# An embedding-mean projection on one core: from the fourth tile's join on, products leave PSUM by VectorE alone

## The chip, the cores and the metric

One core of a Trainium2 chip. The metric is the device time of one execution in microseconds (us); shorter is better. The same core runs everything, so there is no talk between cores.

## The reference

1024 users have 200 item ids each. An id below 12500 is valid; the embedding rows (512 floats) of the valid ids are summed, divided by their number, and the mean goes through a projection with a bias.

```python
valid = sequence_ids < emb_table.shape[0]              # (1024, 200), table (12500, 512)
seq_emb = emb_table[where(valid, sequence_ids, 0)] * valid[..., None]
user_repr = seq_emb.sum(axis=1) / maximum(valid.sum(axis=1, keepdims=True), 1.0)
logits = user_repr @ proj_w + proj_b                   # proj_w (512, 12500), out (1024, 12500)
```

## The kernel before, in words

**Tiles, blocks, units.** The users are 8 tiles of 128; the weights are 25 blocks of 500 columns. A tile times a block is one product, here a unit; there are 200, numbered 0 to 199 in the order in which every engine walks through them (list `units`). The tiles join one after another: tile 0 starts alone at unit 0, and the others join at units 11, 24, 38, 55, 70, 87 and 104 (`joined`, from the argument `JOIN`). A tile that joins begins with the last five blocks that are still there, since five blocks are held at a time (`SPLIT`).

**One unit on TensorE** (lines 839 to 860). Twelve matmuls of 128x128 by 128x500 into one of six PSUM banks (`acc`, unit r uses bank r modulo 6): high halves of mean and weight, then low weight with high mean, then high weight with low mean (`part` 0 to 2, four matmuls each). The first unit of a tile waits for `s_mean_hi` at its start and for `s_mean_lo` ahead of part 2 (lines 844 to 848). A unit first waits until the bank of unit r - 6 is free (`wait_moved`, line 842).

**How a product leaves.** The list `by_act` says for each unit which engine carries it from PSUM to the staging area (`stage`, eleven slots). The two ways differ:

```python
by_act = [r < joined[ACT_TILES] or r < joined[BOTH_TILES] and r % 2 == 0 for r in range(UNITS)]
```

- `by_act[r]` true: TensorE runs a thirteenth, short matmul (line 858) that adds the bias from its three bf16 parts, and ScalarE copies the bank (`move_out`, line 421).
- false: no thirteenth matmul; VectorE adds the bias from `bias_sb` while it copies (`move_out`, line 648). `bias_sb` holds five blocks' biases, each loaded by its own DMA (`load_bias`, line 303) after the last move on VectorE that used its slot (`late_last`).

With `ACT_TILES` 1 and `BOTH_TILES` 5, ScalarE carries units 0 to 10 and then the even ones up to 68: 40 in all.

**VectorE's order is written out by hand** (the loop over `r` in the vector block). For each r: the move of unit r if it is VectorE's; after a join the rest list of the next tile (`fill_slots`); the low halves of a weight block (`w_low`, line 633, two instructions); then the columns of the next tile that are due at r. A tile has 26 columns: gathered embedding rows that are added into `sums` (`add_column`, lines 566 and 569), numbered 0 to 25 here. `column_due` spreads them from joined[t-1] - 2 to joined[t] - t - 3. Between columns stand the sorting rounds of the tile after it (after columns 1, 5, 9, 13 and 17), the rare further sums with their branch after column 20 (`sum_further`), and `choose` after column 19. At joined[t] - 3 comes `mean_of(t)` (line 615), at joined[t] - 2 `mean_low(t)` (line 620). Because the first three columns of the tile after it are due at joined[t] - 2, they and a sorting round stand ahead of `mean_low(t)`.

**TensorE's other steps.** `sum_rest(t)` at joined[t] - 3 (line 794), `turn(t)`, the transposition of the mean (line 774), at joined[t] - 1, after `mean_of(t)`; `list_rest` after the join (lines 786 to 788).

**ScalarE** also rounds the weights to their high halves (`w_high`, line 430), the means (`mean_high`, 446), and scales the rests (`rest_share`, 457).

**GpSimd** gathers the rows by indirect DMA (line 361) into twelve slots. Each pair of gathers waits until the columns that used their slots are added, and, from tile 2 on, for the move of a unit:

```python
if t > 1 and column_due(c) > GATHER_LEAD:
    wait_moved(pool, column_due(c) - GATHER_LEAD - 1)
```

So the first pair of tile 5 waits for the move of unit 47, the first pair of tile 6 for the move of unit 62. `wait_moved` counts the moves of the engine that carries the unit, so it waits for that engine's earlier moves too.

**SyncE** issues the stores (one per unit, line 309), the weight loads (line 297) and the bias loads, in the order of r; each waits on that one queue. From block 16 on there are two slots for raw weights: the load of block 20 follows `w_low(18)`.

Of the kernel before, what the change touches and what calls it, by code (L numbers as in the profile page):

```python
# [5 lines left out]
def mean_embedding_projection(nc, ids, table, proj, bias, out, FAST=26,  # L6
# [24 lines left out]
    RAW_MORE, MORE_LOADS = 2, 16  # L31
    OTHERS_FIRST = 7
    FURTHER_BEHIND, LIST_FIRST_AT, BIAS_DUE = 20, 21, 3
    ACT_TILES, BOTH_TILES = 1, 5
    PART_AT = (0, 32, 64)
    BIAS_ROWS = PART_AT[-1] + NB
    COLS = FAST * TILES
# [845 lines left out]
```

## Time and profile before

| | us |
|---|---|
| median of 3 runs | 633.22 (633.05 to 634.0) |
| the profiled execution | 632.95 |
| its span, first to last instruction | 631.1 |
| TensorE busy (matmuls) | 607.6 (96%) |
| VectorE busy | 407.2 (65%) |
| ScalarE busy | 146.2 (23%) |
| GpSimd busy | 232.2 (37%) |

The profiled execution's own time is its span and some 1.9 us around it. Busy matmul time counts overlapping instructions; the granted clock was 1.00 of full speed, which is the 2.4 GHz level, in all but the start of the span (mean 0.997). Instructions on one engine can overlap by a tenth of a microsecond, so what one costs its engine is best read from start to start. "Idle before" is what the engine waited ahead of an instruction, and for whom.

### The profile page before, as it was taken

Reading aid. Unit: us, or ns where it says so; the run is one execution under the profiler, and the core shown is the slowest. Engines: PE = TensorE matmul, PEld = TensorE weight load, DVE = VectorE, ACT = ScalarE, POOL = GpSimd, SP = SyncE. Lnnn points to the kernel's source line nnn. Section 1 sums busy time; section 2 is a strip of 40 time slices with the busy share of each in tenths; the row PEclk is TensorE's granted clock in tenths of the full one; section 3 lists DMA queues with packets and bytes.
Section 4 is the critical chain, followed back from the end, with each engine's and each line's share of the span. In section 5 each row is a group of like instructions: output and inputs, shape, how many; then the busy total and the mean of one; then the engine's idle time right before and its main releaser. Section 6 shows DMA issues by size and latency. Waiting matters only on the chain.

```text
span 631.1 us, 7599 instructions
## 1 busy us (share of the span) xinstructions
PE 607.6 (96%) x2604; PEld 477.1 (76%) x2604; DVE 407.2 (65%) x721; ACT 146.2 (23%) x163; POOL 232.2 (37%) x227
## 2 busy tenths in 40 slices
PE   1989999999999999999999999999999999999997
PEld 0337657778788777788888888888888888888886
DVE  7988978889896699598698455433333333343442
ACT  8917425132132131120020023111000112111210
POOL 5777877777574377664475000000000000000000
PEclk9989999999999999999999999999999999999999
DMA  9979999999899589888688349935455555566632
GB/s 307 386 259 341 385 393 399 375 320 292 291 319 327 193 279 321 266 251 284 210 285 316 139 133 309 311 120 176 157 179 180 179 169 173 188 186 212 212 112 98
DMA packets 77703, 158.31 MB, mean 251 GB/s; under 512 B 9287, under 2 KB 65042, under 8 KB 77658
## 3 DMA queue, kind: packets, MB, share of 16 engines
q1 hardware_dynamic: 60378, 110.30, 51.0%
q0 software_dynamic: 17280, 47.47, 22.5%
q8 instruction: 21, 0.34, 0.2%
q14 instruction: 24, 0.20, 0.1%
HBM read 115.70 MB, written 51.20 MB: 264 GB/s over the span
## 4 chain that ended last, share of the span: by engine, by line
PE 89%; DVE 5%; DMA 3%; issue 1%; ACT 0%; POOL 0%; POOLq 0%; DVEq 0%
PE acc L853 82%; PE turned L802 4%; DMA rows<-in_L_rec_emb_table_dram,index 3%; DVE sums L569 1%; PE acc L858 1%; DVE w_lo L633 1%; PE turned L794 1%; PE turned L774 0%; DVE top L522 0%; DVE key L526 0%; DMA ids_sb<-in_r_sequence_ids_dram 0%; DVE count L660 0%; ACT w_hi L430 0%; PE turned L788 0%; POOL rows L361 0%
## 5 line engine op out<-in xcount | busy, mean ns | idle before, releaser
L361 POOL DMA_INDIRECT rows<-in_L_rec_emb_table_dram,index x208 | 222.4, 1069 | 101.9 <-issue 60.8
L853 PE MATMUL acc<-w_hi,mean_hi 128*128 128x500 f32 x800 | 224.1, 402 | 0.8 <-ACT mean_hi L446 0.8
L648 DVE TENSOR_TENSOR stage<-acc,bias_sb 128x500 f32<-128x500 f32 x160 | 107.3, 676 | 173.8 <-PE acc L853 173.2
L853 PE MATMUL acc<-w_hi,mean_lo 128*128 128x500 f32 x800 | 213.6, 388 | 0.7 <-DVE mean_lo L620 0.7
L853 PE MATMUL acc<-w_lo,mean_hi 128*128 128x500 f32 x800 | 214.1, 389 | 0.0
L853 PEld LDWEIGHTS acc<-w_hi,mean_lo 128*128 128x128 f32 x800 | 150.3, 188 | 32.1 <-DVE mean_lo L620 1.2
L853 PEld LDWEIGHTS acc<-w_hi,mean_hi 128*128 128x128 f32 x800 | 150.2, 189 | 32.0 <-issue 4.3
L853 PEld LDWEIGHTS acc<-w_lo,mean_hi 128*128 128x128 f32 x800 | 150.3, 188 | 31.5
L569 DVE SCALAR_TENSOR_TENSOR sums<-rows,mask,sums 128x512 f32<-128x512 f32 x165 | 124.2, 753 | 19.5 <-issue 7.3
L430 ACT ACTIVATE w_hi<-w_raw 128x2000 fp32r<-128x2000 f32 x39 | 72.9, 1876 | 220.1 <-PE acc L853 197.7
L633 DVE TENSOR_TENSOR w_lo<-w_raw,w_hi 128x1000 fp32r<-128x1000 f32 x74 | 85.3, 1195 | 13.1 <-ACT w_hi L430 13.1
L421 ACT ACTIVATE stage<-acc 128x500 f32<-128x500 f32 x40 | 23.2, 586 | 93.6 <-PE acc L858 93.6
L457 ACT ACTIVATE mean<-turned,inv_count 128x512 f32<-128x512 f32 x7 | 4.8, 689 | 73.8 <-PE turned L794 65.5
L802 PE MATMUL turned<-rows,diags_at_hi 128*128 128x512 f32 x30 | 15.7, 679 | 1.6 <-DMA rows<-in_L_rec_emb_table_dram,index 1.6
L858 PE MATMUL acc<-bias_parts,pick 89*128 89x500 bf16 x40 | 15.4, 386 | 0.0
L522 DVE MAX8 top<-key 128x8 f32<-128x200 f32 x40 | 14.7, 367 | 0.8
L526 DVE MATCH_REPLACE8 key<-top,key 128x200 f32<-128x200 f32 x40 | 14.3, 358 | 0.0
L802 PEld LDWEIGHTS turned<-rows,diags_at_hi 128*128 128x128 f32 x30 | 6.3, 219 | 10.3 <-issue 6.6
L808 PE MATMUL acc<-many,ones_b 128*128 128x16 bf16 x1 | 0.2, 193 | 12.4 <-DVE stage L667 12.4
L802 PE MATMUL turned<-rows,diags_at_lo 128*128 128x512 f32 x22 | 11.8, 685 | 0.1
L802 PE MATMUL turned<-rows,diag 128*128 128x512 f32 x20 | 9.9, 620 | 1.8 <-DMA rows<-in_L_rec_emb_table_dram,index 1.0
L858 PEld LDWEIGHTS acc<-bias_parts,pick 89*128 89x128 bf16 x40 | 4.1, 102 | 10.0 <-issue 10.0
(106 smaller groups left out, 187.9 us busy)
## 6 DMA issues: line engine op xcount, KB each, us to landing
out_dram<-stage SPq DMA_DIRECT2D x200, 250.0 KB, 3.8
w_raw<-in_L_rec_proj_w_dram SPq DMA_DIRECT2D x39, 1000.0 KB, 7.5
bias_sb<-in_L_rec_proj_b_dram SPq DMA_DIRECT2D x39, 250.0 KB, 5.8
raw_at_hi<-in_L_rec_proj_w_dram SPq DMA_DIRECT2D x4, 1000.0 KB, 14.1
rows<-in_L_rec_emb_table_dram,index POOLq DMA_INDIRECT x208, 6.2
raw_at_lo<-in_L_rec_proj_w_dram SPq DMA_DIRECT2D x3, 1000.0 KB, 16.5
stage<-in_L_rec_proj_w_dram SPq DMA_DIRECT2D x1, 1000.0 KB, 26.1
ids_sb<-in_r_sequence_ids_dram SPq DMA_DIRECT2D x1, 700.0 KB, 4.4
```

Of the source, the lines that this page charges most:

```text
L361: return pool.indirect_dma_start(out=dst, out_offset=None, in_=table, in_offset=bass.IndirectOffsetOnAxis(ap=column, axis=0), bounds_check ...
L421: nc.scalar.activation(stage[:, g % STAGE, r - stores[g][0]], acc[:, r % BANKS, 0:BW], ACT.Copy).then_inc(s_moved_by_act, 1)
L430: nc.scalar.activation(w_hi[:, q % SPLIT], raw(q), ACT.Copy).then_inc(s_w_hi, 1)
L522: dve.max(eight, key[:]).then_inc(s_sort, 1)
L526: dve.match_replace(key[:], eight, key[:], -1.0).then_inc(s_sort, 1)
L569: dve.scalar_tensor_tensor(sums[:], rows[:, c % ROWS], mask[:, t, j:j + 1], sums[:], ALU.mult, ALU.add).then_inc(s_summed, 1)
L633: low = dve.tensor_tensor(w_lo[:, q % SPLIT, at:at + half], raw(q)[:, at:at + half], high, ALU.subtract)
L648: dve.tensor_tensor(stage[:, g % STAGE, r - stores[g][0]], acc[:, r % BANKS, 0:BW], bias_sb[:, i % BIAS], ALU.add).then_inc(s_moved_by_dve, 1)
L794: nc.tensor.matmul(turned[:], placed[:, t % PLACED], rest_rows[:], start=t > 0, stop=t >= len(ON_PE)).then_inc(s_rest, 1)
L802: nc.tensor.matmul(turned[:], diagonal_of(c), rows[:, c % ROWS], start=j == 0, stop=j == FAST - 1).then_inc(s_added, 1)
L853: last = nc.tensor.matmul(bank, first, second, start=part + k == 0, stop=part == 2 and k == K - 1 and not by_act[r])
L858: last = nc.tensor.matmul(bank, pick[:, q % NB:q % NB + 1].to_broadcast([BIAS_ROWS, P]), bias_parts[:], start=False, stop=True)
```

## The change

`BOTH_TILES` goes from 5 to 3. The list `by_act` is now false from joined[3] = 38 on instead of from joined[5] = 70 on. The sixteen even units 38, 40, ... 68 lose their thirteenth matmul (line 858) and are carried by VectorE (line 648) instead of ScalarE (line 421). All waits on their moves go to VectorE's counter, those of TensorE, GpSimd and SyncE alike. Three entries of `late_last` change too, and with each the unit at which a bias load is issued: the bias of block 18 goes from unit 27 to 38, of block 20 from 31 to 40, of block 22 from 37 to 56. The number of bias loads stays 39.

```diff
-    ACT_TILES, BOTH_TILES = 1, 5
+    ACT_TILES, BOTH_TILES = 1, 3
```

## Rows read from the trace of the kernel before

**Rows 1.** The page: the chain that ended last by line; the bias matmul's group.
```profile
PE acc L853 82%; PE turned L802 4%; DMA rows<-in_L_rec_emb_table_dram,index 3%; DVE sums L569 1%; PE acc L858 1%; DVE w_lo L633 1%; PE turned L794 1%; PE turned L774 0%; DVE top L522 0%; DVE key L526 0%; DMA ids_sb<-in_r_sequence_ids_dram 0%; DVE count L660 0%; ACT w_hi L430 0%; PE turned L788 0%; POOL rows L361 0%
...
L858 PE MATMUL acc<-bias_parts,pick 89*128 89x500 bf16 x40 | 15.4, 386 | 0.0
```

**Rows 2.** The chain in order of time: start, length, what (us).
```profile
75.99 1.00 POOL rows L361
...
77.30 6.83 DMA rows<-in_L_rec_emb_table_dram,index
...
183.36 0.23 PE acc L858
...
363.49 264.27 PE acc L853 x1164
```

**Rows 3.** VectorE's timeline up to tile 4's join: start, length, what [idle before].
```profile
177.72 0.22 DVE L584 TENSOR_SCALAR rank<-turned,own_slot 128x1 f32<-128x1 f32 x1 [0.19 <-PE turned L788]
...
195.18 2.31 DVE L633 TENSOR_TENSOR w_lo<-w_raw,w_hi 128x1000 fp32r<-128x1000 f32 x2 [4.92 <-ACT w_hi L430]
...
211.30 0.67 DVE L648 TENSOR_TENSOR stage<-acc,bias_sb 128x500 f32<-128x500 f32 x1
211.89 2.46 DVE L569 SCALAR_TENSOR_TENSOR sums<-rows,mask,sums 128x512 f32<-128x512 f32 x3
214.26 1.26 DVE L648 TENSOR_TENSOR stage<-acc,bias_sb 128x500 f32<-128x500 f32 x2
216.38 0.75 DVE L615 SCALAR_TENSOR_TENSOR mean<-sums,inv_count,mean 128x512 f32<-128x512 f32 x1 [0.86 <-ACT mean L457]
221.29 0.68 DVE L648 TENSOR_TENSOR stage<-acc,bias_sb 128x500 f32<-128x500 f32 x1 [4.16 <-PE acc L853]
221.89 0.75 DVE L566 TENSOR_SCALAR sums<-rows,mask 128x512 f32<-128x512 f32 x1
222.74 0.76 DVE L569 SCALAR_TENSOR_TENSOR sums<-rows,mask,sums 128x512 f32<-128x512 f32 x1
...
226.40 0.68 DVE L620 TENSOR_TENSOR mean_lo<-turned,mean_hi 128x512 fp32r<-128x512 f32 x1
```

**Rows 4.** The same view up to tile 5's join.
```profile
254.75 0.67 DVE L648 TENSOR_TENSOR stage<-acc,bias_sb 128x500 f32<-128x500 f32 x1
...
257.71 1.26 DVE L648 TENSOR_TENSOR stage<-acc,bias_sb 128x500 f32<-128x500 f32 x2
263.86 0.68 DVE L648 TENSOR_TENSOR stage<-acc,bias_sb 128x500 f32<-128x500 f32 x1 [4.89 <-PE acc L853]
...
269.80 0.68 DVE L620 TENSOR_TENSOR mean_lo<-turned,mean_hi 128x512 fp32r<-128x512 f32 x1
```

**Rows 5.** TensorE's timeline, the two joins.
```profile
221.03 0.60 PE L774 MATMUL turned<-ident,mean 128*128 128x128 f32 x4
...
227.13 1.19 PE L853 MATMUL acc<-w_hi,mean_lo 128*128 128x500 f32 x4 [0.74 <-DVE mean_lo L620]
...
266.31 0.39 PE L858 MATMUL acc<-bias_parts,pick 89*128 89x500 bf16 x1
...
271.53 1.08 PE L853 MATMUL acc<-w_hi,mean_lo 128*128 128x500 f32 x4
```

**Rows 6.** GpSimd's timeline: first gathers of tile 5 and of tile 6.
```profile
212.95 1.00 POOL L361 DMA_INDIRECT rows<-in_L_rec_emb_table_dram,index  x1 [8.99 <-DVE sums L569]
...
251.50 1.00 POOL L361 DMA_INDIRECT rows<-in_L_rec_emb_table_dram,index  x1 [0.30 <-issue]
```

**Rows 7.** Landing of single gathers: those begun at 212.95, 214.26, 215.56, and 307.83.
```profile
DMA to landing us min/median/max: 3.5/3.5/3.5
...
DMA to landing us min/median/max: 4.4/4.4/4.4
...
DMA to landing us min/median/max: 5.4/5.4/5.4
...
DMA to landing us min/median/max: 5.5/5.5/5.5
```

**Rows 8.** A stretch with its busy times; last columns: granted clock, DMA share, GB/s.
```profile
183.00:195.00 12.00, 12.00 (x54) 9.46 (x53) 7.08 (x12) 2.32 (x2) 8.37 (x8) 1.00 0.98 351
```

## The prediction, made blind

> **What bounds the kernel now.** I read the chain that ended last first [rows 1]: 82% of it is TensorE's product matmuls. The reader should see there that TensorE is the bound, and that the bias matmul has its own 1%, so it is on the path and not under something. The chain in order of time [rows 2] gives its price: 0.23 us each, 0.227 from start to start (183.36 to 183.59). The 386 ns mean in its group is a pipelined length, not a cost. From 363.49 on the chain is one piece of product matmuls, so what is gained or lost before that reaches the end unchanged, unless a later join adds a wait. Then I read the engine that receives the work, VectorE [rows 3, 4]. It is 65% busy over the span, but what counts is what it does just before tiles 4 and 5 join. TensorE's timeline [rows 5] shows that at tile 4's join it already waits 0.74 us for the low mean, and at tile 5's it does not. Last I read the gathers [rows 6, 7], because their pacing hangs on the moves that change engine.
>
> **The credit.** Sixteen bias matmuls go: 16 x 0.227 = 3.63 us. Nine of them (units 38 to 54) lie before tile 4's join, 2.04 us, seven (56 to 68) between it and tile 5's, 1.59 us. ScalarE loses sixteen copies; it mostly waited for TensorE there, so I cost that at nothing. Should a weight rounding have waited behind a copy, it comes earlier.
>
> **The debit on VectorE.** A move costs it 0.59 us, start to start (211.30 to 211.89 [rows 3]). A column sum directly after another starts 0.85 later, anything else 0.66 later, so a move put between two sums costs only 0.39. Sixteen moves are about 9 us of VectorE, 2.5 times the credit. Whether they matter depends on where VectorE waited.
>
> *Up to tile 4's join.* Moves 38 and 40 fall ahead of the 4.92 us wait at 195.18 [rows 3], which absorbs their own time. But that wait ends with the load of block 20, which is issued after the low halves of block 18, and these now stand behind move 38. The rest list waited 0.19 for TensorE and an instruction may overlap a sum's end by 0.10, so 0.59 - 0.29 = 0.30 us is passed on. Bound below: 0, if the load does not mind. Bound above: the DMA share is 0.98 there at 351 GB/s [rows 8], and two bias loads of 250 KB move towards this stretch while one leaves it: 0.7 us for one, 1.0 in all. I take 0.30, as the first comes 5 us ahead of the load of block 20 and the second behind it.
>
> From there moves 42, 44 (each between two sums) and 46 come ahead of move 47: 0.39 + 0.39 + 0.59 = 1.37. Move 47 goes from 211.30 to 212.97. Then 48 (0.39), 50 and 52 (0.59 each): the mean of tile 4, which could have started at 215.44 and waited until 216.38, starts at 215.44 + 0.30 + 1.37 + 0.39 + 1.18 = 218.68 and ends at 219.43. TensorE finishes unit 53 eight bias matmuls early, at 221.03 - 1.82 = 219.21 [rows 5], so the transposition waits 0.2 us. This alone would be cheap: the 4.16 us that VectorE waited before move 53 are used up, no more.
>
> *The gathers.* The first gather of tile 5 started 0.98 after the end of move 47 (211.97 to 212.95 [rows 6]), so now at 214.62; the next ones follow every 1.30. A row can be used 1.30 after its gather's start (1.00 on GpSimd, then the transfer [rows 2]) plus the landing time. With the landings of these very gathers, 3.5 and 4.4 us [rows 7], the rows are there at 219.42 and 221.62. VectorE reaches column 0 at about 219.9 (move 53, then 0.59) and column 1 at 220.8, where it waits until 221.62. From column 1 to the low mean it needs 226.40 - 222.74 = 3.66 us for sort and sum, so the low mean starts at 225.28. The third row (5.4 us) is there in time. TensorE resumes 0.73 after its start (226.40 to 227.13): 226.01 instead of 227.13. **1.12 us are saved of 2.04 at tile 4's join.** With landings of 5.4 throughout it would be 0.1; with 3.5 throughout 1.96.
>
> *Up to tile 5's join.* VectorE starts 1.12 early. Moves 54, 56, 58 and 60 put move 61 at 254.75 - 1.12 + 2.36 = 255.99 [rows 4]. **Here the pacing changes.** The first gather of tile 6 waits for the move of unit 62, which ScalarE made before; the gather ran at 251.50 [rows 6], without being held up. Now the move stands in VectorE's order, after move 61 and two sums: 255.99 + 0.59 + 0.85 + 0.66 = 258.09, its end 258.76, the gather 259.74. That is 8.2 us later, so tile 6's rows arrive just when VectorE wants them. VectorE itself: after moves 62 to 66 it reaches move 67 at 258.89 - 1.12 + 2.36 + 0.39 + 1.18 = 261.70, where it had waited 4.89; then mean, then move 68 when unit 68 ends, 266.31 - 1.12 - 1.36 = 263.83, plus the 0.27 that such a start lags: 264.10. Column 0 could start at 264.69, column 1 at 265.54. With 4.4 us for the second gather, the row is there at 259.74 + 2.60 + 4.4 = 266.74. The gather at 307.83 is the nearer case, since it too follows a long pause and a run of moves whose stores go out together; it took 5.5 [rows 7], which gives 267.84. The low mean starts 3.66 later, 271.50, and TensorE resumes part 2 at 272.23 instead of 271.53 [rows 5]: **0.70 us later than before**, against 0.40 earlier with 4.4. I take 0.6. Later joins had their order on VectorE before, so nothing is added there, and the end moves with this.
>
> The sum against the profiled execution: 632.95 + 0.6 = 633.55. The median of the runs shown is 0.27 above the profiled one, so the forecast is 633.8. What can be told from no change is about 0.2% (1.3 us), so this is "same", leaning slower.
>
> **A rule of the skill at this point.** The row says 3.5 to 5.5 us landing for a gather of 256 KB. The Trainium skill, "DMA: Bandwidth & Descriptors", section "Anatomy of one DMA — SWDGE (gpsimd) path", fits such a transfer as 2.0 us plus its bytes over 436 GB/s; an estimate from that page is 2.6 us, and by it no row would be late. The trace does not agree: its shortest quoted landing is 0.9 above that.
>
> **Rivals.**
>
> *The rows come in time.* All landings 3.5 us. Tile 4's join saves 1.96; the gather of tile 6 then starts at 258.90, its second row is there at 265.00, hardly after VectorE, which makes unit 68's move at 263.26 and could reach column 1 at 264.70; the low mean follows at 268.66 and TensorE at 269.39: 2.1 us faster, 631.1. For it: the first gather after a pause did take 3.5. Against: the second and third took 4.4 and 5.4. The page's fit would give the same outcome as this rival. The full 3.63 (629.6) would need VectorE to be ahead as well; its order excludes it at tile 5, as the low mean stands behind move 68. Chance 0.17.
>
> *Slower: rows and load late.* The load of block 20 lands 0.7 later still, and the second gathers take 5.4. Tile 5's gather starts at 215.32, its second row is there at 223.32, TensorE resumes at 227.71 (0.58 later); tile 6's gather then starts at 261.44, its second row is there at 269.44, TensorE resumes at 273.83: 2.3 us slower, 635.5. It decides once landings pass 5 us at both joins. For it: the stores of the moves that come in a run now leave together, beside the gathers. The Trainium skill, same page, section "SWDGE vs HWDGE vs iDMA", says that each DMA engine goes round-robin between the two kinds of queue; no row here shows the turns themselves. Against: the DMA queues are nearly empty before tile 5's first gather. Landings near 7 us, as in the start-up [rows 2], would make it about 5 us. Chance 0.30.
>
> *The work was hidden anyway*, so nothing moves and there are no new waits. Against it speaks the bias matmul's own share of the chain. Chance 0.03; the time would be 633.2.
>
> **How the numbers follow.** Forecast 633.8 with chance 0.50. The range takes the rival in time at its lower end with little beyond, 630.9, and the slow one with half a microsecond beyond, 636.1. Within 0.2% lie shifts from -1.3 to +1.3: the forecast, the hidden case and nothing of the other two's cores: 0.53. Faster 0.17, slower 0.30.
>
> **What would show each step.** Line 858: 24 instead of 40, line 648: 176. TensorE's wait before part 2 of unit 55 goes from 0.74 to about 1.7, and a new wait of some 3 us stands before part 2 of unit 70, both for the low mean. VectorE's waits of 4.92 stay near 4; those of 4.16 and 4.89 are gone. Tile 6's first gather starts near 260, after a wait of 8 us or more. VectorE waits for rows ahead of columns 0 and 1 of tiles 5 and 6. No other wait on TensorE after unit 38. It is wrong if TensorE waits for a bank or for block 20 or 21, if the wait at unit 70 is under 1.5, or if the gathers of tile 6 start before 257.

## The result, and the profile after

The changed kernel takes 635.15 us (median of 10 runs, 633.43 to 636.58), the kernel before beside it 633.12 (632.59 to 634.09): ratio 1.0032, 95% interval 1.0025 to 1.0040. It is slower by 2.0 us. That is inside the range of the prediction and outside the 0.2% within which the likeliest case lay. The profiled execution is the fastest of the ten, 633.43 with a span of 631.7, so it does not show all of the loss; a second profile (e1, below) took 635.13 and shows more of it.

The page after, the groups that answer to [rows 1] and to the two ways out:

```profile
L648 DVE TENSOR_TENSOR stage<-acc,bias_sb 128x500 f32<-128x500 f32 x176 | 117.5, 675 | 166.7 <-PE acc L853 166.3
L421 ACT ACTIVATE stage<-acc 128x500 f32<-128x500 f32 x24 | 13.9, 585 | 47.8 <-PE acc L858 47.6
```

Sixteen moves have changed engine, as meant. TensorE's timeline, with the last transposition before the changed stretch (tile 3), those of tiles 4 to 7, and the two waits [rows 5]:

```profile
172.11 0.60 PE L774 MATMUL turned<-ident,mean 128*128 128x128 f32 x4
...
220.35 0.60 PE L774 MATMUL turned<-ident,mean 128*128 128x128 f32 x4
...
226.36 1.18 PE L853 MATMUL acc<-w_hi,mean_lo 128*128 128x500 f32 x4 [0.89 <-DVE mean_lo L620]
...
264.21 0.60 PE L774 MATMUL turned<-ident,mean 128*128 128x128 f32 x4
...
272.06 1.18 PE L853 MATMUL acc<-w_hi,mean_lo 128*128 128x500 f32 x4 [2.71 <-DVE mean_lo L620]
...
315.39 0.60 PE L774 MATMUL turned<-ident,mean 128*128 128x128 f32 x4
...
363.52 0.60 PE L774 MATMUL turned<-ident,mean 128*128 128x128 f32 x4
```

The start of the program differs by up to 2 us between executions (this one reaches tile 3's transposition 0.96 us later than the one before did), so intervals between transpositions say more than spans. In the kernel before the same five lie at 171.15, 221.03, 266.53, 314.77 and 362.90. From tile 3 to 4 the changed kernel needs 48.24 us against 49.88, from 4 to 5 43.86 against 45.50: 1.64 less each. From 5 to 6 it needs 51.18 against 48.24, 2.94 more; from 6 to 7 both need 48.13. In all 191.41 against 191.75: in this execution nearly all of the credit of sixteen bias matmuls is used up by one wait, before part 2 of unit 70, and 0.34 us remain. That its time is still 0.48 above the profiled execution before comes with its start, which is 0.96 us longer.

The chain of waits of the same execution shows how that wait is made:

```profile
258.85 0.68 DVE stage L648
...
260.50 0.38 POOL rows L361
...
261.80 5.90 DMA rows<-in_L_rec_emb_table_dram,index
...
267.73 0.76 DVE sums L569
...
271.31 0.70 DVE mean_lo L620
...
272.06 1.18 PE acc L853 x4
```

The move of unit 62 ends at 259.53, the first gather of tile 6 starts 0.97 later (it started at 251.50 before [rows 6]), the second at 261.80 lands 5.90 later, and VectorE, which waits for it, comes to the low mean of tile 5 only after that row and a sorting round.

The wait has two parts. Put on the time line of the kernel before (0.96 us subtracted), the low mean starts at 270.35, only 0.55 later than the 269.80 of [rows 4]. But TensorE now stands at tile 5's transposition 3.28 us earlier (263.25 against 266.53), and there was about 1 us of slack before: part 2 started 1.73 after the low mean there, where TensorE needs only 0.75 when it waits for it (271.31 to 272.06). 3.28 + 0.55 - 1.0 is 2.8, near the 2.71 shown. The wait is mostly credit that TensorE cannot use, because the low mean did not come earlier with it.

### The profile page after: what moved, and what is told of

The parts are those of the page before. It is cut to its first block, busy times and chain, and to the rows that moved or that the text cites. A ratio compares the mean times of both kernels' runs of the same rounds, so it can differ in the third digit from the quotient of the medians.

```text
span 631.7 us, 7567 instructions
## 1 busy us (share of the span) xinstructions
PE 605.6 (96%) x2588; PEld 477.3 (76%) x2588; DVE 416.1 (66%) x737; ACT 137.3 (22%) x147; POOL 229.4 (36%) x227
## 4 chain that ended last, share of the span: by engine, by line
PE 79%; DVE 8%; issue 5%; DMA 4%; POOL 2%; ACT 1%; DVEq 0%; POOLq 0%
PE acc L853 75%; DMA rows<-in_L_rec_emb_table_dram,index 4%; DVE sums L569 4%; DVE w_lo L633 2%; POOL rows L361 2%; PE turned L802 2%; PE turned L794 1%; ACT rows L406 1%; DVE stage L648 1%; PE acc L858 1%; DVE key L526 0%; PE turned L774 0%; DVE top L522 0%; ACT w_hi L430 0%; ACT L406 0%
## 5 line engine op out<-in xcount | busy, mean ns | idle before, releaser
L361 POOL DMA_INDIRECT rows<-in_L_rec_emb_table_dram,index x208 | 219.9, 1057 | 107.9 <-issue 59.2
L648 DVE TENSOR_TENSOR stage<-acc,bias_sb 128x500 f32<-128x500 f32 x176 | 117.5, 675 | 166.7 <-PE acc L853 166.3
L421 ACT ACTIVATE stage<-acc 128x500 f32<-128x500 f32 x24 | 13.9, 585 | 47.8 <-PE acc L858 47.6
L446 ACT ACTIVATE mean_hi<-turned 128x512 fp32r<-128x512 f32 x8 | 4.8, 596 | 32.2 <-PE turned L774 32.2
L451 ACT ACTIVATE placed<-turned 128x128 f32<-128x128 f32 x6 | 1.7, 278 | 43.6 <-DVE rest_index L591 43.6
```

The source lines that it names most:

```text
L361: return pool.indirect_dma_start(out=dst, out_offset=None, in_=table, in_offset=bass.IndirectOffsetOnAxis(ap=column, axis=0), bounds_check ...
L421: nc.scalar.activation(stage[:, g % STAGE, r - stores[g][0]], acc[:, r % BANKS, 0:BW], ACT.Copy).then_inc(s_moved_by_act, 1)
L648: dve.tensor_tensor(stage[:, g % STAGE, r - stores[g][0]], acc[:, r % BANKS, 0:BW], bias_sb[:, i % BIAS], ALU.add).then_inc(s_moved_by_dve, 1)
```

## The experiments

Intervals from tile 3's to tile 7's transposition are from each run's profile, one execution; ratios are medians of the timed runs against the kernel before, timed beside them.

| run | kernel | ratio (95%) | interval, us |
|---|---|---|---|
| - | before | 1 | 191.75 |
| - | changed | 1.0032 (1.0025 to 1.0040) | 191.41 |
| e1 | changed, again | 1.0030 (1.0014 to 1.0046) | 193.39 |
| e2 | changed, gathers of tile 6 earlier | 0.9967 (0.9954 to 0.9979) | 189.72 |
| e3 | changed, low mean first | 0.9984 (0.9975 to 0.9992) | 189.73 |
| e4 | units 56 to 68 alone | 1.0037 (1.0024 to 1.0049) | 195.55 |
| e5 | units 38 to 54 alone | 0.9973 (0.9962 to 0.9985) | 189.92 |
| e6 | before, gathers of tile 6 after unit 66 | 0.9998 (0.9989 to 1.0007) | 191.66 |
| e7 | before, low mean first | 0.9985 (0.9976 to 0.9994) | 190.65 |
| e8 | changed, e2 and low mean first at tiles 3 to 7 | 0.9982 (0.9973 to 0.9991) | 191.46 |
| e9 | e5 and low mean first | 0.9948 (0.9936 to 0.9961) | 189.31 |
| e10 | before, gathers of tile 6 after unit 67 | 1.0114 (1.0100 to 1.0129) | 197.45 |
| e11 | changed, e2 and e3 | 0.9940 (0.9927 to 0.9953) | 188.78 |
| e12 | e11, means ahead of a move | 0.9942 (0.9927 to 0.9957) | 188.49 |

**e1, the changed kernel again.** No edit.

> The changed kernel once more, for a second profile: the first profiled execution was the fastest of ten, so it may not show what the usual one pays. Theory A (late low mean because of late rows): TensorE waits before part 2 of units 55 and 70 again, together 3.6 us or more, and they grow with the landing times of the first gathers of tiles 5 and 6; the ratio to before is again 1.002 to 1.004. Theory B (something outside these joins, such as a stretch at the lower clock): both waits as in the first profile, 0.9 and 2.7 us, and the difference lies elsewhere in the trace or in the granted clock.

634.81 us, ratio 1.0030. The waits are 0.91 and 3.14 us. TensorE's line after the second, and the busy times of three stretches of it (the column after POOL's is the granted clock, then DMA share and GB/s):

```profile
272.23 1.48 PE L853 MATMUL acc<-w_hi,mean_lo 128*128 128x500 f32 x4 [3.14 <-DVE mean_lo L620]
```

```profile
272.00:274.00 2.00, 1.77 (x7) 1.42 (x8) 1.90 (x4) 0.00 (x0) 1.66 (x2) 0.72 0.85 242
274.00:276.00 2.00, 2.00 (x7) 1.75 (x8) 1.90 (x7) 0.33 (x2) 1.39 (x3) 0.50 0.76 235
276.00:278.00 2.00, 2.00 (x10) 1.65 (x9) 1.88 (x6) 1.72 (x1) 1.70 (x2) 0.92 1.04 302
```

The four matmuls take 1.48 us instead of 1.18, since the granted clock is at its 1.2 GHz level for part of these six microseconds. The work that it withholds is (0.28 + 0.50 + 0.08) x 2 = 1.7 us at full speed. The interval is 1.98 us longer than in the first profile: 1.7 by the clock, most of the rest by the longer wait. So both theories hold: the low mean is late because of late rows (A), and what makes this execution slower than the first profiled one is a stretch at the lower clock (called C in later expectations), which the prediction did not have.

How much of the usual loss is the clock's is shown less well. The mean granted clock is 0.9956 over the nine runs here against 0.9979 over the 28 of the kernel before beside them, which over 634 us would be 1.5 us. But that mean also holds falls in the first 56 us of the program, which come and go: the profiles of e2 and e7 have means of 0.994 and 0.995 with no fall between 56 and 620 us, that of e10 has 0.997 with one. Of the nineteen timed executions of the changed kernel the seven with a mean of 0.997 or more have a median of 634.1 us, the other twelve 635.6. So even the better ones are 1.0 to 1.3 us over the kernel before (633.12, here 632.84), and what makes these slower is not shown by any profile.

**e2, gathers of tile 6 four units earlier.**

```diff
-wait_moved(pool, column_due(c) - GATHER_LEAD - 1)
+wait_moved(pool, column_due(c) - GATHER_LEAD - 1 - (4 if t == 6 else 0))
```

> The changed kernel, but the gathers of tile 6 wait for moves four units earlier (58 instead of 62 for the first pair). Theory A (pacing): the first gather of tile 6 starts near 252 instead of 260.5, VectorE no longer waits for the row of column 1, the wait before part 2 of unit 70 falls from 2.7 to about 1.1 us, and the time falls by 1.6 us or more against the changed kernel. Rival (VectorE is simply overloaded by the moves): the gathers start earlier, but the wait at unit 70 stays within 0.3 us of 2.7 and the time stays.

631.19 us, 0.33% under before, 3.6 us under e1, the changed kernel timed beside it. The wait at unit 70 falls from 2.7 to:

```profile
271.16 1.17 PE L853 MATMUL acc<-w_hi,mean_lo 128*128 128x500 f32 x4 [0.88 <-DVE mean_lo L620]
```

The interval is 1.69 us shorter than in the first profile, as expected, and 3.67 shorter than in e1, whose clock fell; the clock after the wait stays at 1.00 here. One pacing constant turns the change from a loss into a gain, with every move still on VectorE, so load alone was not the cause.

**e3, the low mean of tiles 4 and 5 first.** On VectorE `mean_low(t)` is issued ahead of the columns due at joined[t] - 2 instead of behind them.

```diff
+                for t in (4, 5):
+                    if r + TURN_AHEAD + 1 == joined[t]:
+                        mean_low(t)
...
-                if r + TURN_AHEAD + 1 in joined[1:]:
+                if r + TURN_AHEAD + 1 in joined[1:] and joined.index(r + TURN_AHEAD + 1) not in (4, 5):
```

> The changed kernel, but at tiles 4 and 5 the low mean is computed ahead of the three columns and the sorting round that stood before it. Theory A (the low mean is late because it is queued behind work that needs gathered rows): both waits on TensorE fall under 0.2 us, the whole credit of 3.6 us and the 0.7 us that before paid at tile 4 come through, some 3 to 4 us faster than before. Rival (VectorE overloaded): TensorE waits again somewhere after, for a bank, for weights of block 21 to 24 or for the mean of tile 6, and no more than 1 us is won against before.

631.87 us, 0.16% under before: the two waits for the low mean are gone, but less than half of the expected gain is there. Three small waits on TensorE took their place:

```profile
258.21 1.17 PE L856 MATMUL acc<-w_hi,mean_hi 128*128 128x500 f32 x4 [0.21 <-DVE stage L648]
...
264.56 0.66 PE L777 MATMUL turned<-ident,mean 128*128 128x128 f32 x4 [0.63 <-DVE mean L615]
...
318.71 1.17 PE L856 MATMUL acc<-w_hi,mean_lo 128*128 128x500 f32 x4 [0.64 <-DVE mean_lo L620]
```

The first two, for a bank and for the mean of tile 5, are VectorE's own lateness, now that TensorE no longer loses time. The third is the same mechanism one tile on: the low mean of tile 6 stands behind the first three columns of tile 7, and VectorE waits 0.68, 0.89 and 0.34 us for their rows. By the time, the rival had it right: it allowed a gain of no more than 1 us, and 0.97 was measured. And e7, below, gains 1.12 by the same reordering without the change, so in the timed runs the change itself wins nothing here (0.92 us in the intervals).

**e4, only from tile 4's join on.** `BOTH_TILES` is 4.

> Moves on VectorE alone from tile 4's join on (unit 55), so the even units 38 to 54 stay with ScalarE: BOTH_TILES 4. Theory A by rows: up to tile 4's join all is as before (wait 0.7), then seven bias matmuls less (1.6 us) against a late low mean at unit 70: its wait is 1.5 to 3 us, the end within 1 us of before, a little slower. The second stretch then holds nearly all of the loss. Rival (the first stretch costs it, by the load of block 20 and the transposition): this kernel is 1 us or more faster than before.

635.41 us, ratio 1.0037: with seven moves of the sixteen the whole loss is there, and more than I expected. The wait is 2.05 us, and then:

```profile
272.00:274.00 2.00, 2.00 (x7) 1.55 (x7) 1.83 (x3) 0.00 (x0) 1.70 (x2) 0.50 0.93 231
274.00:276.00 2.00, 2.00 (x8) 1.77 (x8) 1.77 (x6) 0.29 (x2) 1.39 (x3) 0.50 0.88 280
276.00:278.00 2.00, 2.00 (x6) 1.64 (x5) 1.89 (x6) 1.75 (x1) 1.66 (x2) 0.50 1.06 297
278.00:280.00 2.00, 2.00 (x9) 1.60 (x9) 1.23 (x2) 0.54 (x1) 1.43 (x2) 0.84 0.89 263
```

With a granted clock of 0.95 in the two microseconds ahead of these rows, this stretch withholds (0.05 + 0.50 + 0.50 + 0.50 + 0.16) x 2 = 3.4 us. The interval, 195.55, is 3.80 over before; without the clock it would be 0.4 over, which is what the expectation had. The wait is shorter than in the first profile of the change (2.71), and yet the clock fell here and not there.

**e5, only the first stretch.**

```diff
-r < joined[BOTH_TILES] and r % 2 == 0
+r < joined[BOTH_TILES] and r % 2 == 0 and not joined[3] <= r < joined[4]
```

(on the kernel before, with `BOTH_TILES` 5)

> The other part alone: the even units 38 to 54 go to VectorE, units 56 to 68 stay with ScalarE as before. Theory A plus C (late rows at tile 5's join, and a slow clock after the long wait there): nine bias matmuls less, the wait at unit 55 about 0.9 us as in the changed kernel, no wait at unit 70, no fall of the clock after it; 1.5 to 2 us faster than before. Rival (the first stretch makes VectorE late for the second): a wait at unit 70 of over 1 us here too, and no gain.

631.21 us, ratio 0.9973, interval 1.83 under before, with a wait of 0.88 us at unit 55 and none at unit 70. The nine units of the first stretch pay (1.9 us by the medians), the seven of the second cost (2.6 in e4). Together that would be 0.7 us, while the change costs 2.0; why the sum falls short is open.

**e6, late gathers in the kernel before.**

```diff
-wait_moved(pool, column_due(c) - GATHER_LEAD - 1)
+wait_moved(pool, column_due(c) - GATHER_LEAD - 1 + (4 if t == 6 and j < 3 else 0))
```

> The kernel before, with all its bias matmuls and ScalarE's moves, but the first pair of gathers of tile 6 waits for the move of unit 66 instead of 62; nothing else differs. Theory A: the gather starts near 262, the low mean of tile 5 is late by itself, TensorE waits 1.7 to 2.8 us before part 2 of unit 70, with no move added to VectorE. Theory C: after that wait the granted clock falls to 0.5 for some microseconds in most executions, so the time is 3 to 6 us over before, more than the wait; the mean clock of the runs is below that of before. Rival to C (the fall of the clock has another cause, such as the start of the program): the time is over before by the wait alone, 2 to 3 us, and the clocks are as before.

A miss: 632.92 us, ratio 0.9998, no wait at unit 70. The gather does start late, at 261.38, 90.5 us after tile 3's transposition, where the changed kernel's starts 88.4 after its own. The edit (`j < 3`) moves the second pair with it. But the rows land sooner, the second after 3.8 us instead of 5.9. Below are the DMA issues of 258 to 266 us (count, size, median to landing), first of this run, then of the changed kernel:

```profile
out_dram<-stage SPq DMA_DIRECT2D x5, 250.0 KB, 2.4
rows<-in_L_rec_emb_table_dram,index POOLq DMA_INDIRECT x4, 3.9
```

```profile
out_dram<-stage SPq DMA_DIRECT2D x7, 250.0 KB, 4.8
rows<-in_L_rec_emb_table_dram,index POOLq DMA_INDIRECT x5, 5.9
```

VectorE's lines show what that comes to:

```profile
266.49 0.75 DVE L569 SCALAR_TENSOR_TENSOR sums<-rows,mask,sums 128x512 f32<-128x512 f32 x1 [0.91 <-DMA rows<-in_L_rec_emb_table_dram,index]
...
270.30 0.68 DVE L620 TENSOR_TENSOR mean_lo<-turned,mean_hi 128x512 fp32r<-128x512 f32 x1
```

Counted from tile 3's transposition, VectorE goes on with the late row at 95.64 us and starts the low mean at 99.45; in the changed kernel these are 95.62 and 99.20. So the row is just as late in both, the low mean even a little later here, and TensorE waits 2.71 us there and not at all here. What differs is TensorE, which comes to tile 5's transposition at 95.21 here and at 92.10 there. Rows this late cost nothing as long as TensorE is not 3 us ahead; theory A had left out that the slack of the kernel before absorbs them.

In the changed kernel VectorE makes the moves of units 63 to 67 in one run (260.09 to 263.10), their stores leave together with the first gathers, and gathers and stores both take longer. That the run of stores is what lengthens the landing is the reading of these rows, not tested by itself. The Trainium skill, "DMA: Bandwidth & Descriptors", section "SWDGE vs HWDGE vs iDMA", lets each DMA engine go round-robin between the two kinds of queue, which would fit; no run here shows the turns.

**e7, the kernel before with the low mean of tiles 4 and 5 first** (edit of e3).

> The kernel before with the low mean of tiles 4 and 5 ahead of the columns, as in the third run. Theory A: the wait of 0.7 us at unit 55 goes, nothing else; 0.5 to 0.8 us faster than before. Rival: the reordering brings more (over 1.5 us), so the gain of the third run was not the change's.

632.01 us, ratio 0.9985, interval 1.10 us shorter. The wait that the profile gave as 0.74 was worth 1.1; that "idle" counts from a modelled end of the matmul before would explain it, but is not tested. The rival's 1.5 is not reached, but the 1.12 us of the medians are all that e3 won too.

**e8, both cures, the low mean first at tiles 3 to 7.**

> The changed kernel with both cures: gathers of tile 6 four units earlier, and the low mean first at tiles 3 to 7. If the waits of the third run (0.2 for a bank, 0.6 for the mean of tile 5, 0.6 for the low mean of tile 6) come from queueing alone, the last of them goes and 3 to 4 us are won against before. If VectorE is short of time in itself, the wait for the mean of tile 5 stays at 0.5 or more and the gain is about 2.5 us.

632.13 us, ratio 0.9982; neither branch came true. There is one wait, in a new place, for the mean of tile 4:

```profile
222.19 0.66 PE L777 MATMUL turned<-ident,mean 128*128 128x128 f32 x4 [1.91 <-DVE mean L615]
```

At tile 3 the reordering makes VectorE wait for ScalarE's high mean just ahead of the weights of block 18, so the load of block 20 is issued 15.1 us after tile 3's transposition instead of 12.8 in e3, and all of VectorE's first stretch starts late. After the wait the clock falls here too (0.66 over 224 to 228 us). e11, which leaves tiles 3, 6 and 7 alone and has neither this wait nor the fall, bears this out.

**e9, the first stretch with the low mean first** (edits of e5 and e3).

> Only the even units 38 to 54 on VectorE, and the low mean of tiles 4 and 5 first. By rows: nine bias matmuls less (2.0 us) and the 0.7 us wait that before paid at unit 55; no wait at unit 70. From tile 3's to tile 7's transposition TensorE should need 2.8 us less than before, and the time should fall by 2.5 to 3 us. If VectorE's load in the first stretch costs TensorE elsewhere, the interval shows less than 2.2.

630.16 us, ratio 0.9948; the interval is 2.44 us shorter, a little less than expected, as 0.34 us of waiting for the mean of tile 4 appear.

**e10, a long wait in the kernel before.** As e6, with 5 in place of 4.

> The kernel before, with the first pair of gathers of tile 6 behind the move of unit 67, so that TensorE waits long before part 2 of unit 70 while VectorE carries nothing more than before. By rows: gather at 265.5, with landings near 3.8 us the wait is 4 to 5 us. Theory C (a wait of some 3 us or more lets the granted clock fall): the records show a stretch at 0.5 after the wait, and the time is over before by the wait plus about half of that stretch, 6 to 8 us in all. Rival: the clock stays at 1.00 after the wait and the time is over before by the wait alone, 4 to 5 us.

640.37 us, ratio 1.0114, 7.3 us over before. The wait is 4.10 us, and again the clock falls behind it, with nothing changed but the start of the gathers:

```profile
275.41 1.66 PE L853 MATMUL acc<-w_hi,mean_lo 128*128 128x500 f32 x4 [4.10 <-DVE mean_lo L620]
```

```profile
272.00:276.00 4.00, 0.59 (x2) 0.50 (x3) 3.83 (x11) 0.00 (x0) 3.09 (x4) 0.98 0.72 203
276.00:280.00 4.00, 4.00 (x15) 3.31 (x14) 3.76 (x12) 1.04 (x2) 3.08 (x4) 0.59 0.84 244
```

(0.02 + 0.41) x 4 = 1.7 us are withheld; the interval is 5.70 over before, 4.0 by the wait and 1.7 by the clock. This profile is of the fastest of only four timed executions. The fall needs neither the moves nor the missing bias matmuls: here the late gathers bring the wait, and the fall comes behind it.

**e11, both cures at tiles 4 and 5 alone** (edits of e2 and e3).

> The changed kernel, gathers of tile 6 four units earlier, low mean first at tiles 4 and 5 alone (the eighth run did it at tile 3 too, which held back the weights of block 18 and the load of block 20). If that was the eighth run's loss, the load of block 20 is issued as in the third run, the wait for the mean of tile 4 is under 0.3 us, that for the mean of tile 5 near 0.6, and 3 to 4 us are won against before. If the moves make VectorE too late even so, the gain stays at 2 us or less.

629.92 us, ratio 0.9940, 3.2 us under before in the medians, interval 2.97 shorter. The first and second of e3's waits are still there (0.18 and 0.63), the third is gone. Not all of this is the change's: e7 has the same order of the low mean without the change, and against it e11 is 2.1 us better in the medians and 1.87 in the intervals. So with both cures the change is worth about half of its credit of 3.63 us; part of the rest is in the two waits that remain. And e9, with the nine units of the first stretch alone, is not told from e11 by the timed runs (0.9948 and 0.9940, intervals 0.53 apart): nearly all that the change can win lies in the first stretch.

**e12, the means of tiles 4 and 5 ahead of the moves of units 52 and 67.**

> As the run before it, and the means of tiles 4 and 5 ahead of the moves of units 52 and 67. Expected: the wait for the mean of tile 5 falls by the 0.6 us of one move, and the time by as much; 3.5 to 4.3 us under before. If the mean then waits for TensorE's rest sum on VectorE, with the moves of the banks queued behind it, a bank wait appears on TensorE instead and nothing is won.

629.38 us, ratio 0.9942 (0.9927 to 0.9957). The wait for the mean of tile 5 is gone, a wait of 0.18 us for block 21 stands before unit 60, the interval is 0.29 shorter than in e11. The timed runs do not tell it from e11.

## Why the prediction was right or wrong

**The side and the size.** The number was 633.8, the range 630.9 to 636.1, the likeliest case "no change, leaning slower" with 0.50. Measured is 2.0 us slower, a case that had 0.30. The forecast's own sum, 0.6 us, was not what the profiled execution shows either (0.34 faster between the transpositions). That the time of the profiled execution, 633.43, lies so near the forecast's 633.55 for it is luck: its start was 0.96 us longer, and the rest 0.34 shorter. Two terms of the sum were off and one was missing.

**VectorE's order: right.** Times less the 0.96 us offset: move 47 at 212.68 (forecast 212.97), mean of tile 4 at 218.38 (218.68), move 61 at 255.78 (255.99), first gather of tile 6 at 259.54 (259.74), move 67 at 261.5 (261.70). The common 0.2 to 0.3 is the delay passed on through the load of block 20, which did not come: the load landed in 8.9 us instead of 9.5, and the weights' low halves started at 195.20 against 195.18 before. The bias loads that moved towards that stretch cost nothing visible.

**When a row can be used: wrong.** The prediction said "1.30 after its gather's start (1.00 on GpSimd, then the transfer) plus the landing time". The landing time counts from the gather's own start. I had paired the GpSimd row of 75.99 with the transfer of 77.30 [rows 2]; in this run of gathers, one every 1.30 us, a gather starts at 77.30 too, and the transfer is its own. In the chain after, the gather of 261.80 lands after 5.90 and VectorE goes on at 267.73. So at tile 5 no row was late, although landings were 3.8, 5.3 and 5.8 us there: column 1 ran at 222.06, the wait at unit 55 was 0.89 instead of 1.7, and tile 4's join saved 1.73 instead of 1.12.

**The landing at tile 6: too short.** I had 5.5 us for the second gather; it took 5.9, and 6.3 in the second profile. It offsets only a part of the 1.30: the row was there at 266.74 (less the offset), where the forecast's main branch had 267.84. That is the very time of the branch with 4.4 us, which it had worked out and set aside, and by luck: a landing 1.5 us longer, counted from 1.30 earlier, and a gather 0.2 earlier. TensorE resumed part 2 of unit 70 at 271.10, 0.43 before the kernel before, as that branch had it (0.40); the forecast had 0.70 after. In the second profile it resumed at 271.54 on the same time line, level with the kernel before. The mechanism holds: e2 shows the pacing by the move of unit 62, e3 that the waits for the low mean go when it no longer stands behind the rows.

**The price of a wait: the term that was missing.** The sum took a wait on TensorE at its length. "A new wait of some 3 us" was forecast in so many words, and with it there should have been the question what TensorE's clock does behind it. It fell to its 1.2 GHz level in four of the five profiles that have a wait of 1.9 us or more after unit 38 (1.91, 2.05, 3.14 and 4.10; not after the 2.71 of the first profile), and in none of those whose waits stay under 1.1. It cost 1.7 to 3.4 us each time. In the second profile that is the difference from the first: the waits eat up the whole credit (the joins stand level with the kernel before), and the 1.7 us of the clock are the loss. For the median this is likely, not shown: the executions with a high mean clock are also some 1 us over the kernel before. So the number came out inside the range by terms that partly stood in for each other.

**The rivals.** The slow one came closest, 635.5, but by other terms: no late load of block 20, no late rows at tile 5, landings at tile 6 longer than its 5.4 us (5.9 and 6.3), yet rows there 2 us sooner than it had (266.7 and 267.2 against 269.44), and the clock. The fast one needed landings of 3.5 us at all gathers; with the true start of the count they could have been 4.5 us (264.70 - 258.90 - 1.30), still under what the gathers of tile 6 took in the changed kernel, and e2 reached 631.2 by starting the gathers earlier. That nothing would move is refuted by e5.

## What to carry to other kernels

When a step changes its engine, list everyone who waits on that engine's counter, pacing waits too: a throttle that was free because it hung on an idle engine becomes a real wait when the counter moves to a busy one. Put what TensorE waits for ahead of work that needs gathered data on the same queue, and start such gathers with a lead to spare. When work is taken off the busy engine, ask whether what it waits for comes earlier by as much; if not, the credit turns into a wait. Cost a wait of some 2 us or more on TensorE with what the clock may take after it. Take a second profile where the first is the fastest execution; the mean clock of a run does not say where the clock fell. And judge a cure against the kernel before with the same cure, not only against the kernel before.

## What was not expected of the hardware

The granted clock fell from 2.4 to 1.2 GHz in the middle of a program whose TensorE is otherwise 96% busy, after single waits of 1.91 to 4.10 us, for some 3 us in three profiles and some 7 in one, and not after one of 2.71. The Trainium skill, "TensorE: Matmul & The Clock Gate", section "Part 1: The HAM clock gate (the "warmup" mystery)", has the clock set by how busy TensorE has been lately; the runs agree so far as each fall came behind a wait. Which waits let it fall and which don't is not settled by them. The first two gathers of tile 6, all of the same size, landed in 3.3 to 4.4 us in e6 and e10, with five and two stores issued in the eight microseconds around them, and in 4.7 to 6.3 us in the two profiles of the changed kernel, with seven; that the stores are the cause is not tested.
